# A graph network on one core: TensorE takes two additions of the node loops, and VectorE runs them in another order

## The reference, cut to what matters

```python
x = _layernorm(x + L0(x, edge_attr, ..., src, dst))   # edge attention with a segment softmax
x = _layernorm(x + L1(x, edge_index, W_tp, weight, bias))   # bilinear messages
x = _layernorm(x + L2(x, edge_index, ...))   # GIN, two convolutions
x = _layernorm(x + L3(x, src, dst, edge_type, ...))   # typed messages and a GRU

def _gin_conv(x, src, dst, eps, wa, ba, wb, bb, n_nodes):
    agg = jax.ops.segment_sum(x[src], dst, num_segments=n_nodes)
    h = (1.0 + eps) * x + agg
    return jax.nn.relu(h @ wa + ba) @ wb + bb
# L2: h = relu(_gin_conv(x, ... w1a, b1a, w1b, b1b)); h = _gin_conv(h, ... w2a, b2a, w2b, b2b); log_softmax(h)
```

## Time and profile before

| | us |
|---|---|
| median of 3 runs | 4698.01 (4685.06 to 4700.72) |
| profiled execution, its own time | 4688.55 |
| its span | 4686.7 |
| VectorE busy | 3340.9 |
| GpSimd busy | 3240.6 |
| TensorE busy | 2956.8 |
| ScalarE busy | 1618.6 |
| mean granted TensorE clock | 0.703 |

### The profile page before, as it was taken

How to read it: one execution, slowest core, us unless ns; L and a number is a source line. 1 busy time by engine, 2 the same in 40 slices (tenths; PEclk the granted TensorE clock), 3 DMA queues, 4 the chain that set the end, 5 groups by cost and what they waited for, 6 DMA issues and landing times. The chain is left out here.

```text
span 4686.7 us, 58419 instructions
## 1 busy us (share of the span) xinstructions
PE 2956.8 (63%) x13925; PEld 2319.0 (49%) x13925; DVE 3340.9 (71%) x5631; ACT 1618.6 (35%) x4208; POOL 3240.6 (69%) x2831
## 2 busy tenths in 40 slices
PE   5888888888534444435999344473444546777686
PEld 2444444444334444434888234453344436777675
DVE  7999999999795555555888455663556784555678
ACT  3666666666441111102555111121111241222245
POOL 4777777777537888887999677726777337777422
PEclk8777778777665555557999566576556665555688
DMA  4222222222143333343322100031000240000022
GB/s 128 69 67 63 69 69 65 69 63 66 42 135 58 60 60 59 57 76 81 79 78 63 18 7 7 7 93 33 7 7 7 53 114 7 7 7 7 3 74 76
DMA packets 411137, 247.46 MB, mean 53 GB/s; under 512 B 107063, under 2 KB 370091, under 8 KB 410988
## 3 DMA queue, kind: packets, MB, share of 16 engines
q1 hardware_dynamic: 291708, 226.22, 17.4%
q0 software_dynamic: 119296, 19.68, 6.5%
HBM read 180.94 MB, written 64.76 MB: 52 GB/s over the span
## 5 line engine op out<-in xcount | busy, mean ns | idle before, releaser
L1375 PE MATMUL ps<-arena 128*128 128x128 f32 x2976 | 665.7, 413 | 619.3 <-DVE arena L1934 564.6
L771 POOL DMA_INDIRECT extra<-x_t,srci x784 | 767.1, 978 | 260.5 <-issue 245.3
L1375 PEld LDWEIGHTS ps<-arena 128*128 128x128 f32 x2976 | 618.3, 316 | 656.5 <-issue 647.6
L755 POOL DMA_INDIRECT sums<-cmb,sidx x392 | 613.1, 1564 | 136.3 <-issue 117.8
L1248 PE MATMUL ps<-arena,yout 128*128 128x512 f32 x784 | 565.3, 812 | 219.6 <-DVE arena L1725 210.3
L717 POOL DMA_INDIRECT xg<-in_x,xidx x392 | 443.8, 1132 | 203.6 <-issue 118.8
L704 POOL DMA_INDIRECT ft_t<-fts,fidx x392 | 469.2, 1197 | 146.6 <-issue 115.8
L1934 DVE TENSOR_TENSOR arena<-jmask,ps 128x1024 f32<-128x1024 f32 (+1 forms) x174 | 212.5, 1221 | 499.5 <-ACT ps L1030 491.4
L1951 DVE TENSOR_TENSOR arena<-arena,ps 128x128 f32 x1488 | 426.3, 286 | 182.0 <-DVE arena L1951 23.9
L771 POOL DMA_INDIRECT extra<-h_t,srci x392 | 369.9, 944 | 215.5 <-issue 210.9
L1318 PE MATMUL ps<-arena 128*128 128x128 f32 x992 | 224.6, 417 | 445.1 <-DVE arena L1783 347.0
(11 more groups left out here) (257 smaller groups left out, 6407.5 us busy)
## 6 DMA issues: line engine op xcount, KB each, us to landing
edge_in<-in_ef SPq DMA_DIRECT2D x98, 256.0 KB
edge_in<-far_row SPq DMA_DIRECT2D x98, 256.0 KB
ain<-in_src_row SPq DMA_DIRECT2D x56, 448.0 KB, 3.7
sums<-zero SPq DMA_DIRECT2D x132, 144.0 KB
arena<-rel_t SPq DMA_DIRECT2D x63, 256.0 KB, 3.9
x_t<-yout SPq DMA_DIRECT2D x28, 448.0 KB, 3.4
xin<-x_t SPq DMA_DIRECT2D x28, 448.0 KB, 4.0
extra<-x_t,srci POOLq DMA_INDIRECT x784, 2.3
```

The source lines that it names most:

```text
L755: pool.indirect_dma_start(sums[k], bass.IndirectOffsetOnAxis(ap=sidx[n % 2][:, j:j + 1], axis=0), cmb[n % 2][:, j, :], None, compute_op=AL ...
L771: pool.indirect_dma_start(dy[:, t, :], None, table, bass.IndirectOffsetOnAxis(ap=srci[:, t:t + 1], axis=0)).then_inc(d_gathered[n % QUEUE] ...
L1375: last = pe.matmul(slot_sums(k, n)[:, j * P:(j + 1) * P], oneh[b][:, j * P:(j + 1) * P], placed[b][:, j * P:(j + 1) * P], start=True, stop ...
```

## The change

In the first norm TensorE adds the two loaded tiles: it multiplies each by the identity and accumulates both into `ps[3]`, 512 and then 384 columns. VectorE reads the sum from PSUM twice, for the reduction and for the centring; `vv` is not used there. Its order in step t is: reduction of tile t, scaling of tile t - 1, centring of t, the group's expansion, reduction of the squares. SP loads by `v_done`, which TensorE now signals, and ScalarE copies blocks ahead of the square. In the second convolution the output bias comes from a matmul of a tile of ones with three BF16 parts of the bias, which ten small VectorE operations (`split_bias`) make before the bilinear layer; maximum and subtraction read `ps[2]`, and TensorE may refill it after the subtraction. The epsilon sum now runs four tiles ahead and the softmax two, and ScalarE's and SP's orders follow. The core of the diff:

```diff
 SP, gin_stage
-                for t in range(NODE_TILES + 2):
+                ahead = 5 if ph in late_loads else 2
+                for t in range(NODE_TILES + ahead):
                     if t + 2 < NODE_TILES:
                         wait(g_y, NODE_TILES * (ph - 2) + t + 1)
                         load(t + 2)
-                    n = t - 2
+                    if ph in late_loads and 2 <= t < NODE_TILES:
+                        wait(l_t, t - 1)
+                        load_late(t)
+                    n = t - ahead
                     if n < 0:
                         continue
-                    if ph in late_loads and n + 2 < NODE_TILES:
-                        wait(l_t, n + 1)
-                        load_late(n + 2)
...
 SP, first_norm_and_sum_by_source
-                    wait(y_done, t + 1)
+                    wait(v_done, t + 1)
                     load_nodes(t + 2)
...
 ACT, sum_by_source
-                    ready = first_tile_with(0, t)
-                    if ready:
-                        at = block_offsets(0, ready[0])
-                        norm(0, t // 2, t % 2, lambda t=t, n=ready[0], at=at: blocks_of(t, n, at))
-                        copied = ready[0] + 1
-                    else:
-                        norm(0, t // 2, t % 2)
+                    for n in first_tile_with(0, t):
+                        at = block_offsets(0, n)
+                        act.wait_ge(y_done, t)
+                        copy_blocks(0, n, at)
+                        copied = n + 1
+                    norm(0, t // 2, t % 2)
...
 ACT, second convolution
-            for t in range(-3, NODE_TILES):
-                gin_hidden(1, t + 2)
-                gin_turned(1, t + 3)
-                gin_exp(t + 1)
+            for t in range(-4, NODE_TILES):
                 gin_square(t)
-                gin_ln(t + 1)
+                gin_exp(t + 2)
                 gin_factor(t)
+                gin_ln(t + 2)
+                gin_hidden(1, t + 3)
+                gin_turned(1, t + 4)
...
 PE, sum_by_source
-                for n in range(AHEAD + 1):
+                expanded = 0
+                for t in range(NODE_TILES):
+                    wait_loaded(pe, 0, t // 2, t % 2)
+                    if t:
+                        pe.wait_ge(s_xm, t)
+                    for cols in (slice(0, 512), slice(512, W)):
+                        pe.matmul(ps[3][:, cols], ident, xin[t % 2][:, cols], start=True, stop=False)
+                        last = pe.matmul(ps[3][:, cols], ident, ain[t % 2][:, cols], start=False, stop=True)
+                    last.then_inc(v_done, 1)
+                    for n in first_tile_with(1, t):
+                        expand(n)
+                        expanded = n + 1
+                for n in range(expanded, AHEAD + 1):
                     expand(n)
...
 PE, gin_out
                 if t:
-                    pe.wait_ge(g_o, n)
+                    pe.wait_ge(l_zc if q else g_o, t)
                 for g in range(PACKS):
-                    last = pe.matmul(ps[2][:, g * P:(g + 1) * P], hidden[:, g * P:(g + 1) * P], bd[2 * q + 1][:, :],
-                                     start=True, stop=True)
+                    o = ps[2][:, g * P:(g + 1) * P]
+                    if q:
+                        pe.matmul(o, out_ones[:, :], out_bias[:, :], start=True, stop=False)
+                    last = pe.matmul(o, hidden[:, g * P:(g + 1) * P], bd[2 * q + 1][:, :], start=not q, stop=True)
...
 DVE, sum_by_source
-                for t in range(NODE_TILES):
-                    wait_loaded(dve, 0, t // 2, t % 2)
-                    dve.tensor_tensor(vv[:, :], xin[t % 2][:, :], ain[t % 2][:, :], ALU.add).then_inc(v_done, 1)
...
+                v = slots(ps[3][:, 0:W])
+                for t in range(NODE_TILES + 1):
+                    if t < NODE_TILES:
+                        dve.wait_ge(v_done, t + 1)
+                        dve.tensor_reduce(st[:, 0, :], v, AX, ALU.add).then_inc(s_own, 1)
+                    if t:
+                        dve.wait_ge(s_sd, t)
+                        dve.tensor_tensor(slots(x1_of(0, t - 1)), slots(xm[:, :]), over(st[:, 3, :]),
+                                          ALU.mult).then_inc(y_done, 1)
+                    if t < NODE_TILES:
+                        dve.wait_ge(s_own, 2 * t + 1)
+                        if t:
+                            dve.wait_ge(y_done, t)
+                        dve.scalar_tensor_tensor(slots(xm[:, :]), over(st[:, 0, :]), -1.0 / F, v,
+                                                 ALU.mult, ALU.add).then_inc(s_xm, 1)
+                        for n in first_tile_with(1, t):
+                            expand_mask(0, n)
+                            expand_sum(0, n)
+                            expanded = n + 1
+                        dve.wait_ge(s_sq, t + 1)
+                        dve.tensor_reduce(st[:, 1, :], slots(sq_first), AX, ALU.add).then_inc(s_own, 1)
...
 DVE, gin_softmax
-                gin_out(1, t)
-                dve.tensor_reduce(st[:, 6, :], slots(zz), AX, ALU.max).then_inc(l_max, 1)
+                out = slots(ps[2][:, 0:W])
+                dve.wait_ge(g_ops, NODE_TILES + t + 1)
+                dve.tensor_reduce(st[:, 6, :], out, AX, ALU.max).then_inc(l_max, 1)
...
-                dve.tensor_tensor(slots(zcs[t % 2]), slots(zz), over(st[:, 6, :]), ALU.subtract).then_inc(l_zc, 1)
+                dve.tensor_tensor(slots(zcs[t % 2]), out, over(st[:, 6, :]), ALU.subtract).then_inc(l_zc, 1)
...
 DVE, second convolution
-            for t in range(-3, NODE_TILES + 1):
-                gin_ahead(1, t + 3)
+            for t in range(-4, NODE_TILES + 1):
                 gin_scale(t - 1)
-                gin_softmax(t + 1)
                 if t < NODE_TILES:
                     gin_centre(t)
-                gin_sum(t + 1)
+                gin_ahead(1, t + 4)
+                gin_softmax(t + 2)
                 if t < NODE_TILES:
                     gin_squares(t)
+                gin_sum(t + 2)
```

More of the change, by code:

```diff
@@ L255, in build_program @@
         vvs = [vv[:, :], tile_of(13)]
+        out_bias, out_ones = sb("out_bias", [PARTS, P], BF16), sb("out_ones", [PARTS, P], BF16)
+        out_part, out_rest = sb("out_part", [PARTS, PARTS, F], BF16), sb("out_rest", [PARTS, 4, F])
         gate_set = [extra[:, 0:4 * UNIT], arena[:, (N_ACC + 1) * UNIT:(N_ACC + 5) * UNIT]]
@@ L320, in build_program @@
         w_mean, x1_folded, x1b_out = sem("w_mean"), sem("x1_folded"), pair("x1b_out")
+        bias_split = sem("bias_split")
         node_in, late_in, stored = pair("node_in"), pair("late_in"), pair("stored")
@@ L445, in build_program @@
         NODE_PHASES = 5
+        BIAS_MADE = 10
         CONSTANTS = 16 * (5 + PACK + 2)
@@ L961, in step @@
                                    ps[3][:, 512 * b:512 * b + GJ * F], ACT.Copy).then_inc(comb_sb, 1)
-                def blocks_of(t, n, at):
-                    act.wait_ge(y_done, t)
-                    copy_blocks(0, n, at)
                 act.wait_ge(y_zero, 2)
@@ L1467, in _ @@
             sum_by_destination(1)
+            pe.wait_ge(bias_split, BIAS_MADE)
             gin(1)
@@ L1881, in sum_by_source @@
                 expanded = 0
-                for t in range(NODE_TILES):
-                    wait_loaded(dve, 0, t // 2, t % 2)
-                    dve.tensor_tensor(vv[:, :], xin[t % 2][:, :], ain[t % 2][:, :], ALU.add).then_inc(v_done, 1)
-                    ready = first_tile_with(1, t)
-                    if ready:
-                        norm(0, 0, t // 2, t % 2, vv[:, :],
-                             [lambda n=ready[0]: expand_mask(0, n), lambda n=ready[0]: expand_sum(0, n)])
-                        expanded = ready[0] + 1
-                    else:
-                        norm(0, 0, t // 2, t % 2, vv[:, :])
+                v = slots(ps[3][:, 0:W])
[19 more added lines that the diff above has]
+                        dve.tensor_reduce(st[:, 1, :], slots(sq_first), AX, ALU.add).then_inc(s_own, 1)
                 keys(0, 0)
@@ L1895, in sum_by_source, with split_bias @@
                 expand_steps(dve, step)
+            def split_bias():
+                b = prm[0:PARTS, A_B2B:A_B2B + F]
+                part = lambda k: out_part[:, k, :]
+                rest = lambda k: out_rest[:, k, :]
+                at = lambda k: ident[0:PARTS, k:k + 1]
+                dve.memset(out_ones[:, :], 1.0).then_inc(bias_split, 1)
+                dve.tensor_copy(part(0), b).then_inc(bias_split, 1)
+                dve.wait_ge(bias_split, 2)
+                dve.tensor_tensor(rest(0), b, part(0), ALU.subtract).then_inc(bias_split, 1)
+                dve.wait_ge(bias_split, 3)
+                dve.tensor_copy(part(1), rest(0)).then_inc(bias_split, 1)
+                dve.wait_ge(bias_split, 4)
+                dve.tensor_tensor(rest(1), rest(0), part(1), ALU.subtract).then_inc(bias_split, 1)
+                dve.wait_ge(bias_split, 5)
```

(10 more changed lines are left out.)

## The result

| | before | after |
|---|---|---|
| median, 14 runs each | 4694.84 us | 4708.3 us (4701.63 to 4713.94) |
| ratio, 95% interval | | 1.0026 (1.0018 to 1.0033) |
| span of the profiled execution | 4686.7 us | 4706.6 us |
| first norm, start of the first reduction to end of the last scaling | 1283.23 to 1393.66 us | 1282.98 to 1394.01 us |
| second convolution, first epsilon sum to end of the last scaling | 168.9 us | 181.6 us |

The change costs some 12 us by the ratio (the medians are 13.5 apart) where I had forecast a gain of 20. By my bound of 0.3% that is "same", on the slow side, and it lies above the range of 4661 to 4697. The base of my sum, 4698, was the median of three runs, 3.2 us above that of the 14.

A forecast was written before the change was run, and what follows sets the result against it. VectorE was taken to bound both loops; -3.5 us in the first norm and -17 us in the second layer make -20.5 us, from 4698 to 4677.5 us, with a range of 4661 to 4697.

The forecast's parts named there:

- What bounds the kernel: In the first norm and second layer's loop, VectorE bounds the tile; about 1.1 us operations set nose to tail.
- So at most a pass here, 0.24 us slow: Second layer's output: each bias matmul costs at most one pass, 0.24 us at 1.2 GHz; 0 to 1.7 us a tile.
- Fast: hidden. Slow: VectorE waits 1.6 and the tile takes 10.7. I take 9.8: Second layer's tile: output ready at 3.9 us if fast, 6.4 if slow; VectorE asks at 4.8; 9.8 us a tile taken.
- The rival with TensorE's output as the wait: Second layer: each output burst starts slow, 10.7 us a tile, 4689.5 us in all; chance 0.17.
- Floor of 9.1 us a tile, two stalls gone: Second layer: without the bias add and two 1.9 us of waits on GpSimd, plus 0.7, 11.44 us becomes 9.1.
- The prologue, first centring 3.2 us later: Second layer's start: 1.1 us for one more epsilon sum, 2.1 for the second tile's ReLU and copy.
- Second layer's loop -17 us: Second layer: steps of 128 us against 148.6, prologue 3.2 us longer, net -17 us; bounds -26 and -5.
- First norm -3.5 us: First norm: moving the sums to TensorE ends it at 1390.2 instead of 1393.66 us; bounds -9 and +33.
- The ring with one buffer: First norm: VectorE reduces, scales, centres before TensorE writes the next sum into ps[3]; 6.6 us fast, 9.9 slow.
- The rival in which TensorE paces the norm: First norm: sums run at 1.2 GHz, +33 us instead of -3.5, 4714 us in all; chance 0.08.
- The row of 3.35 us: Second layer before the change: after gaps of 3.35 us TensorE starts at the low clock level.
- No extra for reading PSUM: Both loops: PSUM reads cost VectorE nothing more; the skill's 65 ns over 56 reads would mean 3.6 us less gain.

The follow-up runs named there:

- e_nobias: The changed kernel without the second layer's bias matmuls (output bias left out of the result); ratio 0.9944 to the kernel before, loop 143.0 us.
- the grouped form: `e_grouped`: the changed kernel with two wide bias matmuls a tile ahead of the FP32 ones, not seven between them; ratio 0.9949 to the kernel before, loop 148.8 us.
- e_two_sums: The changed kernel with the first norm's sums in two PSUM buffers by turns; ratio 0.9991 to the kernel before.
- e_norm_two: The kernel before with only the first norm's part of the change, its sums in two PSUM buffers by turns; ratio 0.9956 to the kernel before.

## Why the prediction was wrong

Point by point, in its own steps.

- **What bounds the kernel**: right. VectorE bounded both loops, and as soon as TensorE's work was out of its way the tile came down to VectorE's own work (8.8 us between maxima in `e_nobias`).
- **"So at most a pass here, 0.24 us slow"**: this is the step that failed. I took a bias matmul for one more pass in a stream, because it has one weight load and 128 columns, and called that an upper bound. It was not one: 0.47 us a group at 1.2 GHz and 0.31 at 2.4, because the weight loads no longer run through behind it. The outputs took 5.8 us on average, and all but the first took more than the 5.0 that I had as the slow end. I bounded by the nearest row of an unbroken stream. The one row of before with alternation (L1248 to L1250, 512 columns) loses nothing, so it would not have warned me either; what was missing was to call the upper end open.
- **"Fast: hidden. Slow: VectorE waits 1.6 and the tile takes 10.7. I take 9.8"**: 11.6. The rival with TensorE's output as the wait had the mechanism, at a chance of 0.17, but with the same bias term it had 10.7 us. The form of the step held: it starts the output 1.4 us behind the softmax sum and adds every us of output beyond the slack to the tile, which is the ring, though I didn't call it one. With the measured mean of 5.9 us for the output the same step gives 1.4 + 5.9 = 7.3, a wait of 2.5 and a tile of 11.6, which is what came. So the error lies in the output's length alone: 5.9 us, where 3.3 + 1.7 was my slow end and where the 9.8 was a middle between that and an output that is hidden.
- **Floor of 9.1 us a tile, two stalls gone**: right. 9.2 us in the grouped form, and in `e_nobias` seven of 13 distances between maxima are 8.84 us or less; the epsilon sum takes 1.14 us, and the centring, forecast at 1.7 to 1.8 us, takes 1.57 and 1.43 on average with its two buffers.
- **The prologue, first centring 3.2 us later**: too small. From the first epsilon sum to the norm's first reduction it was 29.1 us against 20.3, 8.8 more; the first two outputs are in it. With the bias left out it is 23.8, 3.5 more, so most of the rest goes with the bias matmuls.
- **Second layer's loop -17 us**: +12.7. Prologue 5.6 us off, and 152.5 us from the first centring to the end in place of 128, 24.5 off. The grouped form has -20.1: the size of the forecast, in a kernel that pays for the bias as I thought this one would.
- **First norm -3.5 us**: +0.35. The ring with one buffer and its 7.1 us with an expansion when fast (7.24) are as forecast, as is the last tile (9.1 us from its reduction to the end). But it was 101.9 us between first and last reduction against 95.1; an earlier start (1282.98, not 1286) gave 3.0 back. The larger part, 4.9 us, lies in the four tiles without an expansion, which I had at 7.05 us (the first 7.3) and which took 7.34, 9.49, 8.17 and 8.33. I had counted only that VectorE has less to do there. TensorE has less to do too: its gap before the next sum is 2.49 to 3.47 us, and each of these four sums began at the lower level, while all nine behind gaps of 1.68 or 2.20 us began at the higher. The 8.4 us for a slow tile came true partly by luck: the three tiles of 8.38 to 8.40 us had sums that began fast and fell, where I had them begin slow and recover. The rival in which TensorE paces the norm did not come: the granted clock from 1315 to 1345 us was 0.94. The row of 3.35 us is no rule: in the same loop of before the burst at 3725.99 us, behind a gap of 4.45 us, took 1.02 us, against 1.76 us at the lower level.
- **No extra for reading PSUM**: right by the rows. The maximum reads 128x896 from PSUM in 1.09 us, and the softmax sum reads as much from SBUF in 1.09. The first norm's reduction from PSUM takes 1.09 as well. The extra 65 ns estimated from the Trainium skill's figures (VectorE: DVE Perf Modes, section on the TRN2 errata) do not show. The estimate also counted 56 such reads; the old bias add read PSUM in each tile too, so it is 42 more than before, an estimate of 2.7 us from the same figures.
- **Splitting the bias, nothing**: right. The ten operations run from 2144.11 to 2146.05 us, and VectorE then waits 30.3 us for the bilinear layer's first product.
- **"The savings pass on"**: right. `e_two_sums` and `e_norm_two` show it for the first norm, the grouped form for the second layer; what hides it in a single trace is a spread of several us in the scatter-add stage.

## What to carry to other kernels

A small matmul put between large ones was not priced by its columns here. Look at what it does to the weight loads, and if an accumulator must be started with another operand, start the whole bank once ahead of the stream, instead of alternating. Before calling a producer "hidden", follow its input back: if it depends on the consumer's own last result, the two form a ring, and its slack is a sum over the ring, not a distance in one engine's order. Two cures worked here: a second buffer, and an earlier place for the one operation that the producer waits for. And a tile with less work for the slowest engine is not always the shorter one: it can leave another engine a longer gap and a lower clock.

## What was not expected of the hardware

- A 3x128 bf16 matmul in front of each pair of FP32 passes cost 0.47 us a group at 1.2 GHz; the same seven in a row cost 0.92 us together, 0.13 each, and two of 512 and 384 columns the same 0.92. BF16 matmuls of 128 rows and 512 columns between FP32 pairs lost nothing in the first layer.
- At 2.4 GHz the interleaved output took 4.1 us against 1.83 for the old stream, at 1.2 GHz 6.65 against 3.33. The higher clock did not repair the broken stream.
- TensorE's granted clock from 3716 to 3826 us was 0.66 in the changed kernel and 0.79 with one ScalarE operation placed earlier, with TensorE's own program untouched and its idle time the same. With the grouped bias it was 0.83, with more than twice the idle time.
